# The first expert mixture of a four-layer kernel in one TensorE order: first products in pairs between the neighbour's output tiles

## The reference

```python
capacity = min(max(MIN_CAP, math.ceil(TOP_K * CAP_FACTOR * N / E)), N)     # N = 2048, E = 8: 640
logits = x @ router_w
combine, dispatch = _top2_gating(logits, capacity)
expert_in = jnp.einsum('nec,nh->ech', dispatch, x)
hmid = jax.nn.silu(jnp.einsum('ech,ehf->ecf', expert_in, w1) + b1[:, None, :])     # 128 to 512
expert_out = jnp.einsum('ecf,efh->ech', hmid, w2) + b2[:, None, :]                 # 512 to 128
y = jnp.einsum('nec,ech->nh', combine, expert_out)
shared = jax.nn.silu(x @ sw1 + sb1) @ sw2 + sb2
out = y + SHARED_SCALE * shared
```

## Time and profile before

| | |
|---|---|
| time, median of 3 runs | 1177.18 us (1175.18 to 1180.2) |
| span of the profiled execution | 1195.9 us |
| span less the median of the timed runs | 18.7 us |
| instructions | 18814 |
| mean granted TensorE clock | 0.916 |
| busy | TensorE 85%, VectorE 65%, ScalarE 55%, GpSimd 30% |
| the stage of the change | from 402 to 500 us of the span |

### The profile page before, as it was taken

One profiled execution on the slowest core, in us unless ns is written; L12 is line 12 of the kernel. 1 busy time (PEld: TensorE's weight loads), 2 busy tenths in 40 slices (PEclk: granted clock), 3 DMA queues, 4 the chain that ended last, 5 costly groups with the idle time before them and its releaser, 6 DMA issues.

```text
span 1195.9 us, 18814 instructions
## 1 busy us (share of the span) xinstructions
PE 1013.1 (85%) x6456; PEld 502.9 (42%) x6517; DVE 779.4 (65%) x1614; ACT 662.2 (55%) x1282; POOL 363.6 (30%) x587
## 2 busy tenths in 40 slices
PE   5599789999979899456999999798999998876993
PEld 2267534544436566332333333485323232233551
DVE  5966486768733300388888885429888889646565
ACT  4664536655544345152777777582477776753341
POOL 7535411101532244320000002210112223556554
PEclk9799779999988899865999999898799999999897
DMA  5910224334611120233333220003333423212232
GB/s 142 181 46 1 94 86 144 126 113 129 168 38 36 55 67 18 65 95 126 100 117 125 65 79 5 1 1 126 112 119 119 134 89 96 63 33 62 56 87 80
DMA packets 98374, 101.70 MB, mean 85 GB/s; under 512 B 13354, under 2 KB 80571, under 8 KB 98199
## 3 DMA queue, kind: packets, MB, share of 16 engines
q1 hardware_dynamic: 86169, 89.28, 25.3%
q0 software_dynamic: 6432, 8.18, 2.4%
q10 hardware_dynamic: 5680, 3.04, 0.9%
HBM read 66.60 MB, written 38.09 MB: 88 GB/s over the span
## 4 chain that ended last, share of the span: by engine, by line
PE 67%; DVE 14%; ACT 8%; issue 5%; DMA 3%; another core or an unknown queue 1%; POOL 1%; SPq 0%; ACTq 0%; DVEq 0%; POOLq 0%
PE PS L892 13%; PE PS L876 12%; PE PS L849 8%; PE PS L698 6%; PE PS L703 6%; DVE negm L1663 5%; PE PS L1170 4%; PE PS L1053 3%; PE PS L879 3%; PE PS L1047 2%; PE PS L852 2%; ACT arena L1299 2%; PE PS L900 2%; PE PS L1186 2%; ACT arena L1226 1%
## 5 line engine op out<-in xcount | busy, mean ns | idle before, releaser
L1299 ACT ACTIVATE arena<-PS 128x512 f32<-128x512 f32 (+3 forms) x768 | 363.0, 549 | 190.6 <-PE PS L879 121.8
L1663 DVE TENSOR_REDUCE negm<-PS 128x2 f32<-128x1024 f32 (+3 forms) x384 | 405.2, 1088 | 94.3 <-PE PS L849 46.1
L876 PE MATMUL PS<-arena 128*128 128x512 bf16 (+3 forms) x707 | 221.1, 363 | 12.1 <-ACT arena L1299 8.0
L892 PE MATMUL PS<-arena,VPAD 128*32 128x512 f32 (+3 forms) x1536 | 187.7, 559 | 0.1
L849 PE MATMUL PS<-arena 32*128 32x512 bf16 (+3 forms) x768 | 144.3, 376 | 33.1 <-DVE negm L1663 27.4
L849 PEld LDWEIGHTS PS<-arena 32*128 32x128 bf16 x768 | 36.3, 91 | 216.7 <-DVE negm L1663 112.9
L876 PEld LDWEIGHTS PS<-arena 128*128 128x128 bf16 x768 | 69.9, 98 | 123.5 <-issue 57.3
L2508 POOL CAST nmp<-negm 128x16 bf16<-128x16 f32 x48 | 9.3, 195 | 363.9 <-DVE negm L1663 244.1
L698 PE MATMUL PS<-arena,W 128*128 128x512 f32 x144 | 83.2, 711 | 11.5 <-ACT arena L1217 9.0
L703 PEld LDWEIGHTS PS<-W,arena 128*128 128x128 f32 x640 | 81.0, 206 | 13.8 <-issue 6.3
L703 PE MATMUL PS<-W,arena 128*128 128x128 f32 x640 | 82.8, 291 | 3.3 <-DVE arena L1607 3.0
(11 more groups left out here) (334 smaller groups left out, 1541.3 us busy)
## 6 DMA issues: line engine op xcount, KB each, us to landing
arena<-score_q SPq DMA_DIRECT2D x48, 288.0 KB
arena<-score_k SPq DMA_DIRECT2D x48, 288.0 KB
arena<-max_parts SPq DMA_DIRECT2D x48, 256.0 KB
max_parts<-arena SPq DMA_DIRECT2D x36, 256.0 KB, 2.9
score_k<-arena SPq DMA_DIRECT2D x36, 128.0 KB
score_q<-arena SPq DMA_DIRECT2D x12, 384.0 KB
arena<-rows_y SPq DMA_DIRECT2D x16, 256.0 KB, 4.3
arena<-slots SPq DMA_DIRECT2D x46, 65.0 KB
```

The source lines that it names most:

```text
L876: mm = pe.matmul(PS[:, b, q0:S], OK[s][:, r, kt * P:(kt + 1) * P], OQ[s][:, r, q0:S], start=True, stop=True)
L892: mm = pe.matmul(PS[32 * r:32 * r + 32, 7, q0:S], VP[:, u, kt, r, :], PB[:, kt % 2, r, q0:S], start=(kt == 0), stop=True, skip_group_check ...
L1299: act.activation(PB[:, kt % 2, r, q0:S], PS[:, 4 + use % 3, q0:S], ACT.Exp, scale=slope(u % G, r) if o["slope"] else 1.0).then_inc(exped, 1)
L1663: vec.tensor_reduce(negm[:, u % 2, 2 * rp:2 * rp + 2, qt], PS[:, 2 * (use % 2):2 * (use % 2) + 2, 0:nk], AX.X, ALU.max, negate=True).then_ ...
```

## The change

The two waves give way to one order over the eight experts. On TensorE, expert e's four pairs of first products alternate with the first four output tiles of expert e - 1; the transposes of e + 1 stand behind the second tile, and the fifth tile of e - 1 behind the fourth. ScalarE follows the same order, and issues the load of expert e + 4 behind expert e's Silus. In the last expert each tile gets a step, an add and a wait of its own, and its tiles 1 to 3 go to the A banks of lanes 0 to 2, so that VectorE can read one while TensorE writes the next.

```diff
-                for r in range(2):
-                    for beat, k in wave(3, 1):
-                        ...
+                expert1_turned(0)
+                for e in range(E + 1):
+                    for f in range(4):
+                        if e < E:
+                            expert1_hidden(e, f)
+                        if e > 0:
+                            expert1_tile(e - 1, f)
+                        if f == 1 and e + 1 < E:
+                            expert1_turned(e + 1)
+                    if e > 0:
+                        expert1_tile(e - 1, 4)
+
+            def expert1_hidden(e, f):
+                r, k = divmod(e, B)
+                L = lanes[k]
+                if f == 0:
+                    pe.wait_ge(*A.at(k, f"x{r}.xT4"))
+                for h in range(2):
+                    if f > 0:
+                        pe.wait_ge(*A.at(k, f"x{r}.h{2 * f + h - 2}"))
+                    pe.matmul(PS[:, (L.A, L.B)[h], 0:HALF], W1E[:, e, f * P:(f + 1) * P],
+                              L.exT[:, h * HALF:(h + 1) * HALF], start=True, stop=True).then_inc(*T.did(k, f"x{r}.f{2 * f + h}"))
+
+            def expert1_tile(e, j):
+                r, k = divmod(e, B)
+                if j == 0:
+                    pe.wait_ge(*A.at(k, f"x{r}.h7"))
+                if e == E - 1 and 0 < j < 4:
+                    pe.wait_ge(*V.at(j - 1, "x1.y4"))
+                for f in range(4):
+                    mm = pe.matmul(expert1_out(e, j), lanes[k].eh[:, f, j * P:(j + 1) * P], W2E[:, e, f, :], start=(f == 0), stop=(f == 3))
+                ...
+        def expert1_out(e, j):
+
+            L = lanes[e % B]
+            if e == E - 1 and 0 < j < 4:
+                return PS[:, lanes[j - 1].A, 0:D]
+            return PS[:, L.A if j < 4 else L.B, j % 4 * D:j % 4 * D + D]
 # ScalarE
+                expert1_turned(0)
+                for e in range(E):
+                    for f in range(4):
+                        expert1_hidden(e, f)
+                        if f == 1 and e + 1 < E:
+                            expert1_turned(e + 1)
+                    if e < B:
+                        act.wait_ge(*PO.at(e, "x0.id"))
+                        expert1_rows(e + B)
 # VectorE, the last expert (the others as before)
+                        for j, n in enumerate(("0", "1", "2", "")):
+                            vec.wait_ge(*T.at(k, "x1.o" + n))
+                            vec.tensor_tensor(L.ey[:, j], expert1_out(e, j), eb2[e], ALU.add).then_inc(*V.did(k, "x1.y" + n))
 # GpSimd
-                        pool.wait_ge(*V.at(k, f"x{r}.y4"))
                         for j in range(ET):
+                            pool.wait_ge(*V.at(k, f"x{r}.y4" if (r, k) < (1, B - 1) else ("x1.y0", "x1.y1", "x1.y2", "x1.y", "x1.y4")[j]))
```

More of the change, by code:

```diff
@@ L98 @@
 EXPERTS_A = " ".join(f"x{r}.xT x{r}.xT4 " + " ".join(f"x{r}.h{i}" for i in range(8)) for r in range(2))
-EXPERTS_T = " ".join(f"x{r}.tr " + numbered(f"x{r}.f", 8) + f" x{r}.o x{r}.o4" for r in range(2))
+EXPERTS_T = " ".join(f"x{r}.tr " + numbered(f"x{r}.f", 8) + (" x1.o0 x1.o1 x1.o2" if r else "") + f" x{r}.o x{r}.o4" for r in range(2))
 VECTOR_STEPS = words(" ".join([
@@ L181, in at @@
         return self.sems[c], self.number[c][name]
-def wave(beats, lag):
-    return [(t - lag * c, c) for t in range(beats + lag * (B - 1)) for c in range(B) if 0 <= t - lag * c < beats]
 def taken(steps, turns):
@@ new lines, in experts1, with expert1_turned @@
+                expert1_turned(0)
[9 more added lines that the diff above has]
+                        expert1_tile(e - 1, 4)
+            def expert1_turned(e):
+                r, k = divmod(e, B)
+                L = lanes[k]
+                pe.wait_ge(expert_x[k], 16 * (r + 1))
+                pe.wait_ge(*(V.at(k, "sh.t") if r == 0 else V.at(k, "x0.y4")))
+                for j in range(ET):
+                    t = pe.transpose(PS[:, L.A if j < 4 else L.B, j % 4 * P:j % 4 * P + P], L.ex[:, j, 0:D], ident)
+                t.then_inc(*T.did(k, f"x{r}.tr"))
@@ new lines, in expert1_tile @@
+            def expert1_tile(e, j):
+                r, k = divmod(e, B)
+                if j == 0:
[4 more added lines that the diff above has]
+                    mm = pe.matmul(expert1_out(e, j), lanes[k].eh[:, f, j * P:(j + 1) * P], W2E[:, e, f, :], start=(f == 0), stop=(f == 3))
+                if j == 4:
+                    mm.then_inc(*T.did(k, f"x{r}.o4"))
+                elif j == 3:
+                    mm.then_inc(*T.did(k, f"x{r}.o"))
+                elif e == E - 1:
+                    mm.then_inc(*T.did(k, f"x{r}.o{j}"))
@@ L1384, in experts1 @@
             def experts1():
[L1385 to L1408, removed]
@@ new lines, in experts1 @@
+                for k in range(B):
+                    if k == 0:
+                        for g, tiles in enumerate(GROUP1):
+                            act.wait_ge(scattered[g], 16 * 2 * len(tiles))
+                    act.wait_ge(*T.at(k, "sh.out"))
+                    expert1_rows(k)
+                expert1_turned(0)
[7 more added lines that the diff above has]
+                        expert1_rows(e + B)
@@ new lines, in expert1_rows, with expert1_turned @@
+            def expert1_rows(e):
+                act.dma_start(lanes[e % B].ex, slots_x[e * CAP:(e + 1) * CAP].rearrange("(j p) d -> p j d", p=P)).then_inc(expert_x[e % B], 16)
+            def expert1_turned(e):
+                r, k = divmod(e, B)
+                L = lanes[k]
+                act.wait_ge(*T.at(k, f"x{r}.tr"))
+                act.copy(L.exT[:, 0:512], bank(L.A)).then_inc(*A.did(k, f"x{r}.xT"))
+                act.copy(L.exT[:, 512:CAP], PS[:, L.B, 0:CAP - 512]).then_inc(*A.did(k, f"x{r}.xT4"))
@@ L1410, in void_weights, with expert1_hidden @@
+            def expert1_hidden(e, f):
+                r, k = divmod(e, B)
+                L = lanes[k]
+                for h in range(2):
+                    act.wait_ge(*T.at(k, f"x{r}.f{2 * f + h}"))
+                    act.activation(L.eh[:, f, h * HALF:(h + 1) * HALF], PS[:, (L.A, L.B)[h], 0:HALF], ACT.Silu,
+                                   bias=eb1[:, e, f:f + 1]).then_inc(*A.did(k, f"x{r}.h{2 * f + h}"))
             def void_weights():
@@ L1929, in experts1 @@
                 vec.wait_ge(bias_in, 16 * E)
[L1930 to L1940, removed]
+                for e in range(E):
+                    r, k = divmod(e, B)
+                    L = lanes[k]
+                    if r > 0:
+                        vec.wait_ge(returned[k], 16 * ET)
+                    if e < E - 1:
+                        vec.wait_ge(*T.at(k, f"x{r}.o"))
+                        vec.tensor_tensor(L.ey[:, 0:4], chunk_of(L.A), eb2[e].unsqueeze(1).broadcast_to([P, 4, D]), ALU.add
+                                          ).then_inc(*V.did(k, f"x{r}.y"))
+                    else:
+                        for j, n in enumerate(("0", "1", "2", "")):
+                            vec.wait_ge(*T.at(k, "x1.o" + n))
+                            vec.tensor_tensor(L.ey[:, j], expert1_out(e, j), eb2[e], ALU.add).then_inc(*V.did(k, "x1.y" + n))
+                    vec.wait_ge(*T.at(k, f"x{r}.o4"))
+                    vec.tensor_tensor(L.ey[:, 4], PS[:, L.B, 0:D], eb2[e], ALU.add).then_inc(*V.did(k, f"x{r}.y4"))
             def cleared_values():
```

6 lines of the change are left out of this document (3 added, 3 removed).

## The result

| | before | changed |
|---|---|---|
| time, median of 6 runs, taken together | 1176.95 us (1171.03 to 1180.2) | 1163.59 us (1160.82 to 1169.6) |
| span of the profiled execution | 1195.9 us | 1159.1 us |
| first product to combine, in the two traces | 101.8 us | 91.4 us |

The ratio is 0.9894, with a 95% interval of 0.9868 to 0.9919, or 9.5 to 15.5 us less. In the traces the stage is 10.3 us shorter (101.76 to 91.42), where the prediction had 9.0.

The account below looks back on a forecast made before the run. TensorE was taken to bound the stage, stalled by Silu waits. Its end came 10.9 us earlier, 1.9 given back to GpSimd's scatters: 1177.2 - 9.0 = 1168.2 us, with range 1165 to 1174.5 for 8 in 10.

Parts of the forecast that it names:

- The bound: Mixture stage: TensorE sets the pace, busy 77.83 of 82 us, with weight loads waiting 19.2 us for ScalarE's Silu.
- Starts behind a satisfied wait cost nothing: TensorE's alternations: each start costs 0, upper bound 0.10 us, so a block takes 9.41 us.
- late weights: Rival, 8%: nine alternations a block each cost 0.10 us; block 10.3 us, gain 2.7 us, time 1174.5 us.
- the slower rival: Rival, 4%: TensorE can't load weights past waits; 14 starts a block cost 0.19 us each; 9.6 us lost, 1187 us.
- ScalarE behind the transposes: Pair behind the transposes has 0.36 us slack; rival, 6%: no slack, blocks stand up to 0.5 us, gain about 5.5 us.
- Start and turn: Expert 1 starts at 411.8 us, seven blocks of 9.41 us follow, then expert 7's tiles; TensorE ends 10.9 us earlier.
- The tail: Stage end: GpSimd has ten scatters in a row, 1.284 us apart; 1.9 of 10.9 us given back, gain 9.0 us.
- the single gating: Expert 7's scatters each wait for their own add: worth nothing, since GpSimd is busy with expert 6 until 485.4 us.
- Behind it: From last scatter to combine and attention 2: memset's slack grows from 3 to 5 us; the 9.0 us reach the end.
- given back later: Rival, 6%: stage ends 9 us earlier, but gathers or attention 2's maxima wait as long as before; 1176 us.
- Sum: Gain 74.9 - 7p, 9.0 us at block p = 9.41; timed runs 18.7 us below the span, so 1168.2 us.

Follow-up runs that it names:

- the two repeats: The changed kernel run again without edit, twice, each against the kernel before: 1183.74 us, ratio 0.9893, and 1187.06 us, ratio 0.9918.
- before_again: The kernel before, unedited, profiled once more: span 1179.1 us, timed 1180.84 us in that execution.
- singles_from5: The changed kernel with single adds and scatter waits for experts 5 to 7, not 7 alone: 1184.81 us, 0.9911 to before; again 1185.99 us, 0.9916.

## Why the prediction was right or wrong

- *The bound.* Right. In the stage TensorE set the pace, and the alternation fills the bubbles behind the waits for Silu. The 19.2 us are the waits of weight loads, in part under running matmuls; what TensorE gained is 12.1 us up to expert 7's tiles (84.42 to 72.36 from the first product).
- *Starts behind a satisfied wait cost nothing.* Right: 9.32 us a block leaves no room for 0.10 us anywhere. The Trainium skill (TensorE: Matmul & The Clock Gate, LDWEIGHTS) has a load of 128 columns at an estimate of 0.107 us, and had all nine alternations of a block exposed one, the block would have been 10.3 us, by that estimate. The trace shows none of them exposed, so late weights fell, and with it the slower rival.
- *ScalarE behind the transposes.* The slack was there: the pair behind the transposes (451.14) is followed by a tile at 452.22 and the next pair at 453.11, both at the stream's own pace.
- *Start and turn.* Here is the failed step, mis-sized: "Seven blocks follow: 411.8 + 7 x 9.41 = 477.7". From the first product to expert 7's tiles that is 73.57 us, and the trace has 72.36 (392.39 to 464.74, before rounding). The last of the seven blocks has no transposes, as there is no expert 8; it took 8.77 us, and 0.55 us were counted that don't exist. And the step of a tile's record was worked out wrongly from my own rows: forty take 4.57 us, and less the 0.10 of the first that leaves 4.47, or 0.112 a step, not 4.54 and 0.1135. Five tiles of a block stream in 4.47 us (0.89 each), whether they alternate or not: expert 7's forty in a row, 4.63 us with the 0.28 of the last record, are 39 steps of 0.112 too. The rows of before thus gave a block of 9.34, where 9.32 was measured; 0.09 in each of seven blocks is 0.63, and together it is 1.2 us. The first 7.67 us, expert 0 with expert 1's transposes set among its products, came out at 7.67 (to 400.06), with luck: the granted clock rises in it, from 0.50 up to 396 us to 1.00 from 398, and the two repeats took 7.27 and 7.24.
- *The tail.* Right in its mechanism and its terms: ten scatters, 1.28 us apart, the first 1.33 us behind expert 6's last tile (464.74 to 466.07), and the single gating worth nothing. It gave back the 1.9 us that the sum said. The last scatter started 85.2 us behind the first product in place of the forecast 86.5, which is the 1.2 us from above handed on. The repeats reach 85.2 and 85.3 otherwise: expert 7's tiles start 0.4 us sooner, and the first scatter 1.73 and 1.81 us behind.
- *Behind it.* Right: the memset moved with TensorE's end (6.88 us from 471.36) and left 5.02 us of idle before the combine, where I had written about 5; gathers and attention 2 followed the combine (given back later fell). The granted clock at TensorE's restart was 0.50 (490 to 496 us), as before.
- *Sum.* The base was sound only by luck. I took the surplus of the profiled span over the timed runs for a constant of the kernel; before_again shows that it is none. The stage was the same in all three traces of before within 0.9 us (101.4 to 102.3), so a sum of differences within it could be carried over. With 10.3 us in place of 9.0 it gives 1166.9, inside the range and inside the first measurement's interval (0.9868 to 0.9919 of 1177.18 is 1161.6 to 1167.6). The rest, 3.3 us down to 1163.59, no run tells from chance: the other two measures of the change gave 12.8 and 9.8 us.

So the mis-sized blocks are 1.2 us of the miss, and alone they wouldn't have put the time outside the range. The range's low end, 1165, was only 3.2 us below the forecast: it held the block of 9.3 us (by the prediction's own formula 9.8 us of gain, 1167.4), but neither a last block that lacks a part nor the scatter of a measurement, which the same prediction puts at 5.9 us. Whether something outside the stage gained in the first measurement stays open.

## What to carry to other kernels

Where one engine's products wait for another's eviction, put independent work of a neighbour between them; the gain is the time in which the first engine's stream stood, less what the next engine then has to work off in one go at the end. So count the queue at the end of a stage (ten scatters at 1.28 us here), and let it start tile by tile from early on, not just in the last iteration: that was worth another 4.5 us at the combine in one pair of traces and 2.7 in another. When a sum multiplies a block by its count, write out the first and the last one separately.

## What the runs showed of the hardware that was not expected

The same instruction list has a span some 15 to 28 us longer in one trace than in another (before: 1179.1, 1193.9 and 1195.9; changed: 1159.1, 1182.4 and 1187.6), though the stage takes the same time in each within 0.9 us. The timed runs bear it out: the median of 17 runs of before was 1178.16 us on one chip, and 1196.38 and 1197.46 on two others. Where the traces differ, ScalarE and VectorE stand idle, often together, for 1 to 6.5 us with no releaser in the trace. The last column of the table falls into two groups, 675 to 678 us and 687 to 696 us. All nine traces of the longer group have such waits between 1070 and 1130 us, and none of the five of the shorter one has. They come at the same few lines in one kernel, and both traces of singles_from5 have some in the rewritten stage as well. In the windows from 1080 to 1110 TensorE is busy for 20.18 us in the first trace of before, at a granted clock of 0.85,

```profile
1080.00:1110.00 30.00, 20.18 (x95) 11.68 (x96) 18.01 (x73) 8.42 (x21) 19.64 (x30) 0.85 0.23 65
```

and for 27.69 us, at 1.00, in before_again:

```profile
1080.00:1110.00 30.00, 27.69 (x150) 17.05 (x148) 22.81 (x81) 12.32 (x29) 22.85 (x37) 1.00 0.33 86
```

A late fetch of the engines' own instructions would fit stalls at fixed instructions, and the Trainium skill (Runtime: NRT & Kernel Launch, Instruction fetch mechanics) has an engine's instructions fetched in blocks ahead of their execution and calls the cost "mostly hidden". The kept traces speak against it. The page of before lists 93 packets in two queues of the kind instruction over the whole span; the queues from 1092 to 1112 us, with all six stalls of over 2 us, are these, and none of that kind is among them:

```profile
q1 hardware_dynamic: 1629, 0.76, 15.0%
q0 software_dynamic: 416, 0.84, 12.2%
```

It is the same from 462 to 472 us in singles_from5, so no late fetch landed at the end of these stalls. Their cause stays open. Whether singles_from5 runs without its stall in a place with the shorter span wasn't tried: its second run, meant to tell, was on a chip with the longer one.

A second thing: VectorE's memset of 6.88 us beside GpSimd's scatters left their pace at 1.28 us, in the changed kernel as in the one before.
